# New instruction orders for the first and last sequences of a 32-sequence decoder layer, and where ScalarE's tables are loaded

## The chip, the core and the metric

The kernel runs on one core of a Trainium2 chip. The metric is the device time of one execution in microseconds (us). A core has five engines that each work through their own list of instructions in order: TensorE (PE, matrix products), VectorE (DVE), ScalarE (ACT), GpSimd (POOL) and SyncE (SP), which here only issues transfers. They are tied together by semaphores alone.

## The reference, cut to what matters

For each of 32 sequences of 128 tokens and 512 channels, one decoder layer is computed:

```
x = x + Wo( groupnorm(rwkv(LN(x))) * silu(g) )      # projections r, k, v, g of token-shift mixes of LN(x)
x = x + softmax(q k^T / 4) v                        # q = LN(x), k = v = ctx, 32 heads over 8 KV heads
x = x + FFN(LN(x))                                  # W1, gelu, W2; inputs and weights quantised to
                                                    # MXINT8 in blocks of 32, LN and output in bf16
```

The linear attention works in chunks with a per-head decay; its state runs inside one sequence only, so the sequences do not depend on each other. They share the weights: five float32 matrices of 512x512, and W1 (2048x512) and W2 (512x2048), which the kernel quantises itself, once, in 16 pieces.

## The kernel before

The whole kernel is a software pipeline over sequences n = 0 to 31. Each engine's block defines small helpers (one step of one sequence: `stats_q(n)`, `project("r", n, ...)`, `scores_max(n, i)`) and then calls them in an order that is written out by hand: a long straight list for the first sequences, a loop `for n in range(10, 27)` for the middle, and another straight list for the last ones. At one time about six sequences are in flight. In one pass of the loop the engines do steps of sequences n, n - 1, ... n - 5. Nothing sorts the work at run time: an instruction that waits holds up everything behind it on its engine.

The steps that the prediction speaks of, with their lines in the kernel before:

- Load and quantise a weight piece (16 pieces, 512 KB each, in two buffers `wst`): SP `load_w12(n)` (L200) waits until piece n - 2 is quantised (`dve_w_q`); VectorE `w12_scale(n)` takes block maxima (L1739, L1660, L1666, L1667); GpSimd `w12_scaled(n)` multiplies (L3292); VectorE `w12_quantise(n)` rounds (L1747, L1751); SP `w12_turned(n)` transposes by DMA (L266).
- First LayerNorm: VectorE `stats_q(n)`, `norm_mv("q", n)`; ScalarE `rstd_log`, `rstd_exp` (a logarithm and an exponential) and `normalise_q(n)` (L2529, writes `xx`); TensorE `turn_x(n)` transposes it (L516, waits for `act_xn`); ScalarE `x_turned(n)`; VectorE `differences(n)` (L1553); then `mixed` for k and v on VectorE, for r and g on GpSimd; then the projections.
- The decay masks `wm`, once: `distances(i)` (L1758), ScalarE `decays(i)`, GpSimd `bonuses(i)` (L3301), `bonus_added(i)` (L1764).
- Projection out: VectorE `scaled_y`, `gated_y` (L1597, L1601), TensorE `project_out(n)` (L599), VectorE `first_sum(n)` (L1608). Then the cross-attention: `normalise_x` (L2536), `turn_queries` (L605), `queries_x` (writes `qdense`, L2612), `scores_max` (L614), `maxima` (L1614), `scores_x`, `weights_x`, `values_x`, `out_odd` (L2642), `turn_sums`, `turn_out`, `normalise_o` (L1630, writes `x2`, whose buffer must have been stored two sequences before).
- Feed-forward: `hidden...` steps, `up(n, j)` (L654), `gelu(n, j)`, `gelu_max`, `gelu_pow2`, `gelu_scale` (GpSimd, L3282), `gelu_round`, `gelu_quantised` (L1719), a DMA transpose, `down(n, i)` (L663), `second_out`, `last_sum`, `store`.

ScalarE can hold one table of functions at a time. The steps with a logarithm or exponential need `TABLE_EXP`, `gelu` and `gate_tanh` need `TABLE_GELU`; the plain copies and scalings (`normalise_q`, `queries_x`, `x_turned`, `out_odd`) run under either. The loads are written into the order as `e.preload_act_table_set(...)`.

In the middle loop of the kernel before, ScalarE's order around the second LayerNorm reads:

```
gelu(n - 4, 1); out_odd(n - 3); <load TABLE_EXP>
rstd_log("x", n - 2); rstd_exp("x", n - 2); normalise_x(n - 2)
rstd_log("q", n); rstd_exp("q", n); normalise_q(n); queries_x(n - 2); x_turned(n)
<load TABLE_GELU>; gate_tanh(n - 1); gate_in(n - 1)
```

## Time and profile before

| | |
|---|---|
| Three timed runs | 1359.17, 1360.65, 1353.01 us; median 1359.17 |
| Profiled execution, span from first to last instruction | 1355.6 us |
| TensorE busy | 1249.7 us (92%), mean granted clock 0.968 |
| VectorE busy | 1134.3 us (84%) |
| ScalarE busy | 823.1 us (61%) |
| GpSimd busy | 636.6 us (47%) |
| DMA | 97.09 MB, mean 72 GB/s |

The page gives the profiled execution by its span alone; no other time of it is shown. "PE" is TensorE's products, "PEld" its weight loads, which overlap with them. L-numbers are lines of the kernel before; helpers are called for every sequence, so a line stands for one step of all sequences. "Idle before" is the time in which the engine had nothing to do ahead of a row, with what ended it. A granted clock of 1.00 is 2.4 GHz and 0.50 is 1.2 GHz.

### The profile page before, as it was taken

The numbers are of one execution on the slowest core, as the hardware profiler recorded it, in microseconds if no ns is written. First come the engines' busy times: TensorE is split into PE (matmuls) and PEld (weight loads), VectorE is DVE, ScalarE is ACT, GpSimd is POOL, SyncE is SP. The second block draws the span as 40 slices with busy tenths as digits, with TensorE's granted clock in tenths as the row PEclk, the third lists the DMA queues.
The fourth block names the chain that finished last, engine by engine and source line by source line (L and its number), as shares of the span: only waits on it lengthen the run. The fifth ranks groups of instructions, "written<-read, shape, count | busy, mean of one in ns | idle before, by whom it ended". The sixth has DMA issues, their size and how long they took to land.

```text
span 1355.6 us, 34643 instructions
## 1 busy us (share of the span) xinstructions
PE 1249.7 (92%) x13352; PEld 797.8 (59%) x13352; DVE 1134.3 (84%) x1960; ACT 823.1 (61%) x1577; POOL 636.6 (47%) x700
## 2 busy tenths in 40 slices
PE   1677989999999999999999999999999999999744
PEld 1564666656666666566666666666666666666411
DVE  5889978888888887888888888888888888888875
ACT  1334475766666666666666666667666666666641
POOL 3756444544445445544445455444445454443322
PEclk8789999999999999999999999999999999999976
DMA  9335312222222223222212233222212322221212
GB/s 323 101 95 136 67 39 73 70 71 57 51 57 61 63 67 70 70 70 49 56 50 64 65 70 70 71 70 50 56 52 64 63 71 69 70 59 38 67 49 51
DMA packets 137332, 97.09 MB, mean 72 GB/s; under 512 B 108113, under 2 KB 110161, under 8 KB 136401
## 3 DMA queue, kind: packets, MB, share of 16 engines
q1 hardware_dynamic: 137168, 94.87, 27.8%
q8 instruction: 107, 1.75, 0.6%
q14 instruction: 57, 0.46, 0.1%
HBM read 37.16 MB, written 8.39 MB: 34 GB/s over the span
## 4 chain that ended last, share of the span: by engine, by line
PE 79%; DVE 10%; issue 4%; DMA 2%; POOL 2%; ACT 1%; SPq 1%; POOLq 0%; DVEq 0%; ACTq 0%
PE bank_b L547 15%; PE bank_y L599 8%; PE bank_a L547 8%; PE bank_y L663 7%; PE bank_a L537 7%; PE rt L566 5%; PE rt L614 4%; PE rt L627 4%; PE bank_o L633 4%; PE bank_b L654 4%; PE bank_a L654 4%; PE bank_o L593 2%; PE bank_y L585 2%; PE bank_y L580 1%; DVE negm L1614 1%
## 5 line engine op out<-in xcount | busy, mean ns | idle before, releaser
L3282 POOL TENSOR_TENSOR gmem<-gmem,unit_g 128x1024 bf16<-128x1024 bf16 x64 | 124.1, 1940 | 214.1 <-DVE unit_g L1667 214.1
L1614 DVE TENSOR_REDUCE negm<-rt 128x16 f32<-128x2048 f32 x64 | 146.2, 2284 | 2.3 <-PE rt L614 1.5
L663 PE MATMUL bank_y<-w2q,gmem 128*128 128x512 bf16 x512 | 122.4, 393 | 19.3 <-DMA gmem<-gmem 19.3
L2626 ACT ACTIVATE pT<-rt 128x2048 f32<-128x2048 f32 x64 | 120.0, 1875 | 28.1 <-PE rt L627 20.3
L547 PE MATMUL bank_a<-mix_r,w_Wr 128*128 128x128 f32 x1024 | 124.3, 280 | 5.6 <-POOL mix_r L3241 5.6
L547 PEld LDWEIGHTS bank_a<-mix_r,w_Wr 128*128 128x128 f32 x1024 | 118.5, 194 | 16.1 <-issue 10.1
L547 PE MATMUL bank_b<-mix_k,w_Wk 128*128 128x128 f32 x1024 | 122.1, 278 | 5.2 <-DVE mix_k L1560 5.2
L3273 POOL TENSOR_TENSOR gt<-gt,yT 128x512 f32<-128x512 f32 x32 | 41.1, 1285 | 181.0 <-ACT yT L2604 181.0
L547 PEld LDWEIGHTS bank_b<-mix_k,w_Wk 128*128 128x128 f32 x1024 | 120.5, 196 | 7.2 <-issue 7.2
L547 PE MATMUL bank_b<-mix_g,w_Wg 128*128 128x128 f32 x1024 | 122.0, 278 | 0.0
L547 PEld LDWEIGHTS bank_b<-mix_g,w_Wg 128*128 128x128 f32 x1024 | 118.6, 194 | 2.0 <-issue 1.6
L599 PE MATMUL bank_y<-w_Wo,yT 128*128 128x512 f32 x256 | 115.4, 593 | 1.3 <-DVE yT L1601 1.3
L537 PE MATMUL bank_a<-w_Wv,mix_v 128*128 128x512 f32 x256 | 115.5, 594 | 0.1
L1585 DVE TENSOR_TENSOR att<-rt,wm 128x1536 f32<-128x1536 f32 x64 | 112.1, 1751 | 2.9 <-PE bank_y L585 1.4
L663 PEld LDWEIGHTS bank_y<-w2q,gmem 128*128 128x128 bf16 x512 | 50.1, 100 | 86.6 <-issue 27.5
L3266 POOL TENSOR_TENSOR gh<-gt,half_ln 128x512 f32<-128x512 f32 x32 | 52.3, 1635 | 77.3 <-DVE gt L1592 77.3
L2578 ACT ACTIVATE gt<-bank_b,half_bg 128x128 f32<-128x128 f32 x128 | 36.5, 370 | 79.7 <-PE bank_b L547 79.7
L537 PEld LDWEIGHTS bank_a<-w_Wv,mix_v 128*128 128x128 f32 x256 | 48.2, 190 | 61.9 <-issue 59.9
L566 PEld LDWEIGHTS rt<-rz,kT 32*64 32x64 f32 x3072 | 63.1, 131 | 34.0 <-issue 25.2
L3237 POOL TENSOR_SCALAR mix_r<-xx,all_columns 128x128 f32<-128x128 f32 x128 | 49.6, 406 | 65.0 <-DVE xx L1553 65.0
L1719 DVE SCALAR_TENSOR_TENSOR gmem<-gmem,pow_g 128x1024 bf16<-128x1024 f16 x64 | 79.2, 1238 | 1.1
L599 PEld LDWEIGHTS bank_y<-w_Wo,yT 128*128 128x128 f32 x256 | 48.2, 190 | 54.0 <-issue 49.1
(205 smaller groups left out, 2829.8 us busy)
## 6 DMA issues: line engine op xcount, KB each, us to landing
qx<-qdense SPq DMA_DIRECT2D x64, 224.0 KB, 3.1
context<-ctx SPq DMA_DIRECT2D x32, 384.0 KB, 3.3
xin<-x SPq DMA_DIRECT2D x32, 256.0 KB, 3.2
gmem<-w SPq DMA_DIRECT2D x16, 512.0 KB, 4.0
out<-x SPq DMA_DIRECT2D x32, 256.0 KB, 2.9
vp<-vz SPq DMA_DIRECT2D x32, 128.0 KB
odense<-oT SPq DMA_DIRECT2D x128, 32.0 KB, 1.9
pT<-Wv SPq DMA_DIRECT2D x1, 1024.0 KB, 8.1
```

The lines of the kernel that those rows point to most:

```text
L537: done = e.matmul(bank_a[:, :], mix["v"][:, c, :], wt["Wv"][:, c, :], start=(c == 0), stop=(c == KT - 1))
L547: done = e.matmul(bank[:, m * T:(m + 1) * T], wt[f"W{name}"][:, c, m * P:(m + 1) * P], mix[name][:, c, :], start=(c == 0), stop=(c == KT - 1))
L566: done = e.matmul(rtb(g)[HALF * side:HALF * side + HALF, at:at + (q1 - q0) * HALF], kT[rows32, m, HALF * keys:HALF * keys + HALF], rz[rows ...
L599: done = e.matmul(bank_y[:, :], yT[:, c, :], wt["Wo"][:, c, :], start=(c == 0), stop=(c == KT - 1))
L614: done = e.matmul(rtb(g)[:, jj * 2 * T:(jj + 1) * 2 * T], qdense[rows32, 2 * i + jj, :], kd[n % 2][rows32, :, :], start=True, stop=True)
L654: done = e.matmul(bank[:, :], hqT[:, c, :], w1q[:, 4 * j:4 * j + 4, c, :], start=(c == 0), stop=(c == KT - 1))
L663: done = e.matmul(bank_y[:, :], gqT[:, t, :], w2q[:, t, :], start=(t == 0), stop=(t == FT - 1))
L1585: e.tensor_tensor(att[:, :, :, :, :].rearrange("p g m k t -> p g (m k t)"), rt[:, :].rearrange("p (g n) -> p g n", g=4)[:, :, 0:6 * HALF], ...
L1614: e.tensor_reduce(negm[:, 0:H].rearrange("p (g a j) -> p g j a", g=4, a=2)[:, :, 2 * i:2 * i + 2, :], rt[:, :].rearrange("p (g j a s) -> p ...
L1719: e.scalar_tensor_tensor(blocks(half), blocks(half.bitcast(FP16)), MAGIC16, per_block(pow2[f"g{i}"], 32), ALU.subtract, ALU.mult).then_inc ...
L2626: e.activation(pT[:, :, :].rearrange("p g n -> p (g n)"), rt[:, :], ACT.Exp, scale=float(D) ** -0.5).then_inc(sem(f"act_ex{i}"), 1)
L3282: e.tensor_tensor(blocks(half), blocks(half), per_block(unit[f"g{i}"], 32), ALU.mult).then_inc(sem(f"pool_gsc{i}"), 1)
```

## The change

Every helper's arithmetic is as before; no instruction on the data is added or taken away. Changed are:

- the straight lists ahead of and behind the loops, on all five engines;
- the ranges of the loops (TensorE 7 to 26, VectorE 9 to 26, ScalarE 9 to 27, GpSimd 8 to 31, SP 10 to 27; before 10 to 26 on all), each beginning at another step of the pass. Taken round in a circle, the order of the steps in the pass is the same as before on all engines;
- the places of ScalarE's table loads. In the kernel before a load stands right ahead of the first step that needs the table, after it right behind the last step that needed the other one. This holds inside the loop too. Over the whole kernel there are 12 loads fewer;
- one added wait, of `project_out(0)` for the load of `Wo`.

```diff
@@ SP, start
-            load_x(0)
-            load("masks", masks[:, :], masks_in)
-            load("columns", all_columns[:, :, :], columns)
-            load("heads", per_head[:, :], heads)
-            load_w12(0)
             load_w12(1)
-            load("Wv", wv_rows, weights["Wv"])
-            load("b1", b1row[:, :], b1)
-            for k in ROWS:
-                load("rows", row[k][:, :], rows[k])
+            load("Wo")
+            load_row("bo")
             load_x(1)
...
+            load("Wv")
+            load("Wk")
             load_w12(2)
             load_w12(3)
+            load("Wr")
             w12_turned(1)
+            w12_turned(0)
+            load_row("ffn_ln_w")
+            load("Wg")
             load_w12(4)
...
@@ ScalarE, middle loop
-            for n in range(10, 27):
+            for n in range(9, 28):
...
                 e.preload_act_table_set(TABLE_GELU)
                 gelu(n - 4, 0)
                 gelu(n - 4, 1)
+                e.preload_act_table_set(TABLE_EXP)
                 out_odd(n - 3)
-                e.preload_act_table_set(TABLE_EXP)
                 rstd_log("x", n - 2)
                 rstd_exp("x", n - 2)
                 normalise_x(n - 2)
                 rstd_log("q", n)
                 rstd_exp("q", n)
+                e.preload_act_table_set(TABLE_GELU)
                 normalise_q(n)
                 queries_x(n - 2)
                 x_turned(n)
-                e.preload_act_table_set(TABLE_GELU)
                 gate_tanh(n - 1)
                 gate_in(n - 1)
```

VectorE, from the rounding of weight piece 2 back to the first LayerNorm's statistics, before (`amax_w`, `pow_w`, `unit_w` are block maxima of a weight piece, `hz` and `hw` the two buffers of quantised pieces, `xx` the result of `differences(0)`):

```order
L1739 TENSOR_REDUCE amax_w<-gmem 128x32
L1660 TENSOR_SCALAR amax_w<-amax_w 128x32
L1666 TENSOR_SCALAR pow_w<-amax_w 128x32
L1667 TENSOR_SCALAR unit_w<-amax_w 128x32
L1521 BN_STATS stats_q<-xin 128x6
L1529 BN_AGGR mv_q<-stats_q 128x2
L1532 TENSOR_SCALAR shift_q<-mv_q 128x1
L1521 BN_STATS stats_q<-xin 128x6
L1747 TENSOR_SCALAR gmem<-gmem 128x1024
L1751 SCALAR_TENSOR_TENSOR hz<-gmem,pow_w 128x1024
L1553 TENSOR_TENSOR xx<-xT 128x512
```

and after:

```order
L1374 BN_AGGR mv_q<-stats_q 128x2
L1377 TENSOR_SCALAR shift_q<-mv_q 128x1
L1366 BN_STATS stats_q<-xin 128x6
L1374 BN_AGGR mv_q<-stats_q 128x2
L1377 TENSOR_SCALAR shift_q<-mv_q 128x1
L1592 TENSOR_SCALAR gmem<-gmem 128x1024
L1596 SCALAR_TENSOR_TENSOR hz<-gmem,pow_w 128x1024
L1592 TENSOR_SCALAR gmem<-gmem 128x1024
L1596 SCALAR_TENSOR_TENSOR hw<-gmem,pow_w 128x1024
L1398 TENSOR_TENSOR xx<-xT 128x512
```

Before, the maxima of pieces 2 and 3 and the rounding of pieces 0, 1 and 2 stand ahead of `xx`; after, only pieces 0 and 1 do (their maxima stand further up), and `distances(1)` and `bonus_added(0)` come later too.

ScalarE in the middle loop, before, from the load that follows `out_odd`:

```order
L2961 ACT_TABLE_LOAD
L2510 ACTIVATE logv_x<-mv_x,eps 128x1
L2517 ACTIVATE rstd_x<-logv_x 128x1
L2521 ACTIVATE shift_x<-shift_x,rstd_x 128x1
L2536 ACTIVATE xq<-x_1,shift_x,rstd_x 128x512
L2510 ACTIVATE logv_q<-mv_q,eps 128x1
L2517 ACTIVATE rstd_q<-logv_q 128x1
L2521 ACTIVATE shift_q<-shift_q,rstd_q 128x1
L2529 ACTIVATE xx<-xin,shift_q,rstd_q 128x512
L2612 ACTIVATE qdense<-rt 128x512
L2561 ACTIVATE xT<-bank_o 128x4x128
L2970 ACT_TABLE_LOAD
```

and after:

```order
L2728 ACT_TABLE_LOAD
L2449 ACTIVATE oT<-bank_o 128x512
L2317 ACTIVATE logv_x<-mv_x,eps 128x1
L2324 ACTIVATE rstd_x<-logv_x 128x1
L2328 ACTIVATE shift_x<-shift_x,rstd_x 128x1
L2343 ACTIVATE xq<-x_1,shift_x,rstd_x 128x512
L2317 ACTIVATE logv_q<-mv_q,eps 128x1
L2324 ACTIVATE rstd_q<-logv_q 128x1
L2328 ACTIVATE shift_q<-shift_q,rstd_q 128x1
L2735 ACT_TABLE_LOAD
L2336 ACTIVATE xx<-xin,shift_q,rstd_q 128x512
L2419 ACTIVATE qdense<-rt 128x512
```

The first load has moved from behind `oT` (`out_odd`) to ahead of it, the second from behind `xT` to ahead of `xx` (`normalise_q`).

VectorE shortly before the last `project_out`, before (`yT` is first `scaled_y(31)`, then `gated_y(31)`):

```order
L1689 SCALAR_TENSOR_TENSOR hz<-hz,pow_h 128x512
L1719 SCALAR_TENSOR_TENSOR gmem<-gmem,pow_g 128x1024
L1655 TENSOR_REDUCE amax_g<-gmem 128x32
L1597 TENSOR_TENSOR yT<-bank_y,gt 128x512
L1660 TENSOR_SCALAR amax_g<-amax_g 128x32
L1666 TENSOR_SCALAR pow_g<-amax_g 128x32
L1667 TENSOR_SCALAR unit_g<-amax_g 128x32
L1601 TENSOR_TENSOR yT<-yT,gh 128x512
```

and after:

```order
L1442 TENSOR_TENSOR yT<-bank_y,gt 128x512
L1529 TENSOR_SCALAR hz<-hz 128x512
L1446 TENSOR_TENSOR yT<-yT,gh 128x512
L1534 SCALAR_TENSOR_TENSOR hz<-hz,pow_h 128x512
L1564 SCALAR_TENSOR_TENSOR gmem<-gmem,pow_g 128x1024
L1500 TENSOR_REDUCE amax_g<-gmem 128x32
```

The two steps of sequence 31 now stand ahead of the last rounding of the hidden layer and of the quantising of sequence 28's gelu.

## Rows read from the trace of the kernel before

**Rows 1.** Head of the page: span, and busy time of each engine.
```profile
span 1355.6 us, 34643 instructions
...
PE 1249.7 (92%) x13352; PEld 797.8 (59%) x13352; DVE 1134.3 (84%) x1960; ACT 823.1 (61%) x1577; POOL 636.6 (47%) x700
...
```

**Rows 2.** Windows: stretch, length, busy us (count) of PE, PEld, DVE, ACT, POOL; PEclk.
```profile
0.00:204.00 204.00, 144.62 (x1573) 103.78 (x1573) 168.62 (x252) 88.98 (x176) 107.80 (x112) 0.88 0.46 128
600.00:900.00 300.00, 300.00 (x3265) 193.99 (x3263) 254.88 (x457) 200.78 (x391) 147.65 (x168) 1.00 0.25 62
1254.00:1356.00 102.00, 60.70 (x435) 26.02 (x430) 72.75 (x125) 41.61 (x67) 28.96 (x19) 0.80 0.24 55
```

**Rows 3.** Timeline of VectorE, 0 to 90 us: start, length, engine, line, operation, [idle before].
```profile
6.17 2.67 DVE L1772 TENSOR_SCALAR per_head<-per_head 128x48 f32<-128x48 f32 x1 [1.25 <-ACT per_head L2672]
...
17.08 2.80 DVE L1751 SCALAR_TENSOR_TENSOR hz<-gmem,pow_w 128x1024 bf16<-128x1024 f32 x1
...
20.52 1.23 DVE L1751 SCALAR_TENSOR_TENSOR hw<-gmem,pow_w 128x1024 bf16<-128x1024 f32 x1
...
32.24 1.22 DVE L1739 TENSOR_REDUCE amax_w<-gmem 128x32 f32<-128x1024 f32 x1 [8.83 <-DMA gmem<-w]
...
40.76 0.69 DVE L1553 TENSOR_TENSOR xx<-xT 128x512 f32<-128x512 f32 x1 [0.66 <-ACT xT L2561]
...
58.20 0.69 DVE L1572 TENSOR_TENSOR vz<-bank_a,bv_row 128x512 f32<-128x512 f32 x1 [2.44 <-PE bank_a L537]
...
88.19 0.69 DVE L1608 TENSOR_TENSOR x<-bank_y,xin 128x512 f32<-128x512 f32 x1 [3.63 <-PE bank_y L599]
```

**Rows 4.** Timeline of the DMA-issuing queue, 0 to 30 us.
```profile
19.91 5.98 SPq L266 DMA_TRANSPOSE w1q<-hz  x1
...
25.94 1.05 SPq L200 DMA_DIRECT2D gmem<-w  x2
```

**Rows 5.** Timeline of TensorE, 0 to 60 us.
```profile
45.67 5.48 PE L547 MATMUL bank_a<-mix_r,w_Wr 128*128 128x128 f32 x32 [5.57 <-POOL mix_r L3241]
```

**Rows 6.** Timeline of ScalarE, one pass of the middle loop.
```profile
712.78 0.60 ACT L2642 ACTIVATE oT<-bank_o 128x512 f32<-128x512 f32 x1 [2.55 <-PE bank_o L633]
...
713.39 1.28 ACT L2961 ACT_TABLE_LOAD   x1
...
714.69 0.29 ACT L2510 ACTIVATE logv_x<-mv_x,eps 128x1 f32<-128x1 f32 x1
...
716.80 0.29 ACT L2510 ACTIVATE logv_q<-mv_q,eps 128x1 f32<-128x1 f32 x1 [0.35 <-DVE mv_q L1529]
...
717.75 0.81 ACT L2529 ACTIVATE xx<-xin,shift_q,rstd_q 128x512 f32<-128x512 f32 x1
...
718.47 0.58 ACT L2612 ACTIVATE qdense<-rt 128x512 f32<-128x512 f32 x1
...
720.80 1.28 ACT L2970 ACT_TABLE_LOAD   x1
```

**Rows 7.** Timeline of TensorE, same pass.
```profile
719.49 0.66 PE L516 MATMUL bank_o<-masks,xx 128*128 128x128 f32 x4
...
720.08 1.15 PE L614 MATMUL rt<-context,qdense 32*128 32x256 f32 x16
```

**Rows 8.** Timeline of ScalarE, then TensorE, an earlier pass.
```profile
526.09 0.82 ACT L2529 ACTIVATE xx<-xin,shift_q,rstd_q 128x512 f32<-128x512 f32 x1
...
527.37 0.66 PE L516 MATMUL bank_o<-masks,xx 128*128 128x128 f32 x4
```

**Rows 9.** Timeline of the last 100 us: VectorE three, ScalarE one.
```profile
1270.45 2.30 DVE L1719 SCALAR_TENSOR_TENSOR gmem<-gmem,pow_g 128x1024 bf16<-128x1024 f16 x1
...
1273.80 0.68 DVE L1597 TENSOR_TENSOR yT<-bank_y,gt 128x512 f32<-128x512 f32 x1
...
1315.16 0.69 DVE L1630 TENSOR_TENSOR x<-bank_o,rden 128x512 f32<-128x512 f32 x1 [1.09 <-DMA out<-x]
...
1280.96 1.28 ACT L3192 ACT_TABLE_LOAD   x1
```

More of the change, by code:

```diff
@@ L1105, in _ @@
+            for n in range(7, 27):
                 e.wait_ge(sem("dve_ze0"), n - 3)
@@ L1780, in _ @@
             w12_quantise(1)
[L1781 to L1788 removed]
+            differences(0)
+            distances(1)
+            mixed(0, "v")
+            w12_scale(2)
+            mixed(0, "k")
+            w12_quantise(2)
+            w12_scale(3)
+            bonus_added(0)
+            w12_scale(4)
             w12_quantise(3)
[L1790 removed]
@@ L2276, in _ @@
+            up_out(25, 2, bank_a)
+            gelu_round(25, 0)
+            denominators(26)
+            differences(29)
+            residual(24)
+            maxima(27, 0)
+            mixed(29, "v")
             normalise_o(26)
-            maxima(27, 1)
+            decayed(28, 1)
             stats_f(26)
+            gate(28)
+            gelu_quantised(25, 0)
+            gelu_max(25, 1)
             norm_mv("f", 26)
-            maxima(27, 0)
+            scaled_y(28)
+            gated_y(28)
```

2255 lines of the change are left out of this document (948 added, 1307 removed).

## The prediction

> **What bounds the kernel now.** I read the page's head first. TensorE is busy 1249.7 of 1355.6 us, VectorE 1134.3 [rows 1]. The reader is to ask where the missing 106 us of TensorE lie. The windows answer: there are three stages, each with its own limit [rows 2]. From 600 to 900 us TensorE is busy 300.00 of 300: it alone sets the pace, VectorE has 15% to spare. In the first 204 us TensorE is busy 144.62, which leaves 59.4 us idle, and VectorE 168.62: VectorE, which quantises the weights beside its usual work, is nearer to its limit. In the last 102 us TensorE idles 41.3 us and VectorE 29.3: no engine is full, and the chain of sequence 31 sets the end. The amount of TensorE work is the same in both kernels, so the new time is the old one less the idle time taken out of head and tail, plus whatever idle time appears in the middle, where each microsecond that TensorE waits is a microsecond of the kernel.
>
> The sum is made against the span of 1355.6 us. The page shows no other time of that execution; the three timed runs lie between 1353.01 and 1360.65, so I add the sum to their median, 1359.17, and keep some 3 us for that spread. This measurement can tell about 0.5% (6.8 us) from no change.
>
> **The head: less idle time on VectorE.** VectorE's timeline shows waits of 1.25, 8.83, 0.66, 2.44 and 3.63 us on the way to the first `first_sum` [rows 3]. The largest is for weight piece 2: the SP queue issues seventeen other transfers, then the transpose of piece 0 holds it from 19.91 to 25.89, and only then come the loads of pieces 2 and 3, for which VectorE waits until 32.24 [rows 3, 4]. Sequence 0's LayerNorm stands behind those pieces on VectorE, so `xx` starts at 40.76 and TensorE's first projection at 45.67 [rows 3, 5]. In the new order, pieces 2 and 3 are loaded ahead of any transpose, with b1, three rows and Wg behind them, and the LayerNorm stands behind pieces 0 and 1 alone. What is only moved gains nothing, since VectorE has to do it anyway; what counts are the waits. 8.83 + 0.66 go, because piece 2 is now issued as soon as piece 0 is quantised. That was at 19.88 here (`hz`, 17.08 + 2.80) and should be near 19; with the 6.3 us from 25.94 to 32.24 it lands by 25.3, and VectorE, which first has `xx`, `distances(1)` and `mixed(0, "v")` to do, asks for it at about 26 (an estimate). The 1.25 goes, since piece 0's maxima now stand ahead of the rates. New are a wait for piece 0 to land and one for ScalarE's rstd ahead of the second `norm_mv`, which I estimate at 1.2 us together. That is 9.5 us. Of the other two waits, 2.44 + 3.63, I take half, 3.0. Head: -12.5 us. TensorE then starts near 26 to 28 us instead of 45.67, which is more than VectorE's gain, so VectorE stays the limit and not TensorE. Bounds: 4 us, if other waits take half of it and the later weight pieces come late (each load still waits for the piece two before); 20 us, which is the whole shift of the first projection.
>
> One cost is in this already: a VectorE operation can be held for as long as a GpSimd one runs. `hz` took 2.80 us at 17.08 and its twin `hw` 1.23 at 20.52, and the 48 wide `per_head` took 2.67 [rows 3]. The new order has as many such pairs, at other places; I count 0, with 2 us either way.
>
> **The middle: the table load that moved.** The loop's steps keep their order on every engine, but on ScalarE both loads inside the pass have moved. The first, of 1.28 us at 713.39, goes ahead of `oT` (712.78), where ScalarE was idle for 2.55 us: it is hidden, and brings `logv_x` forward, which nobody waits for, as the next step `logv_q` is held until 716.80 by VectorE anyway [rows 6]. The second, at 720.80, stood where ScalarE then had nothing to do. It now stands between `shift_q` and `xx` (717.75), with `qdense` behind it. So `xx` ends at 717.75 + 1.28 + 0.81 = 719.84 instead of 718.56. TensorE's `turn_x` needs it and started at 719.49 [rows 7]: there was 0.93 us in hand in this pass, 0.46 in the pass at 527.37 [rows 8]. Those are the ends of nine passes that I looked at, seven of them above 0.78; I take 0.8. The new wait is 1.28 - 0.8, or 0.5 us. Nothing catches it up: the input of `logv_q` comes from VectorE, whose list hangs on this pass's `project_out`, so the whole pass slides. `qdense` ends 0.6 after `xx`, at 720.4, and `scores_max` starts behind `turn_x` at 720.08 + 0.5: covered by 0.1. The ScalarE loop has 19 passes (9 to 27): 19 x 0.5 = +9.5 us. Bounds: 0, if a slack that the trace doesn't show takes it; 19 x 1.28 = 24.3, if the slack in front of `turn_x` is not there.
>
> The row of 713.39 is followed by `logv_x` at 714.69, 0.02 after the load ends, and it starts 0.01 after `oT` [rows 6]. The Trainium skill (ScalarE: Activation LUTs, What ACT_TABLE_LOAD costs) gives 1283 ns for the load and another 1380 ns of drain, 2.66 us for a switch. The trace shows the first and not the second. By the page the wait in each pass would be 1.9 us and the middle would lose 36 us; I go by the rows.
>
> **The tail.** Four pieces, each read from a wait or an order. (a) `scaled_y(31)` (the `yT` row) is now ahead of `gmem` and `amax_g`, which filled the time from 1270.45 to 1273.80 [rows 9]; part of these 3.35 us is GpSimd's own arrival, so I take 2.4. (b) The load ahead of the last LayerNorm x, 1.28 us at 1280.96, stood behind `out_odd` on the chain; now it is done earlier: 1.3. (c) `normalise_o(31)` waited 1.09 us for the store of sequence 29 [rows 9]; `down(29, 1)` now stands ahead of `up(30)`, so that store is earlier: 1.1. (d) `gelu_quantised(30, 0)` has moved behind `hidden(31)`, and `second_out(30)` behind the last maxima: 0.7. Tail: -5.5 us. The two `down(30)` halves now stand behind `up(31)`; they run while TensorE waits for the last gelu, which it did before too. Bounds: 0 and 10.
>
> **Sum.** -12.5 + 9.5 - 5.5 = -8.5 us. 1359.2 - 8.5 = 1350.7 us.
>
> **The rivals.**
>
> A, the middle stays free: something ahead of `turn_x` has slack that hides the moved load. For it: TensorE's ends are modelled, and `turn_x` is never seen waiting in the middle. Against: 0.5 to 0.9 us in hand against 1.28. Time: 1359.2 - 18 = 1341.
>
> B, the head gives little: the loads of later pieces, which still wait two by two for VectorE, put the saved 9 us back as waits further on, and the middle costs its 9.5. For it: between 40 and 80 us VectorE's one long wait is the 2.44, so it has no reserve for a late piece. Against: the DMA queue is lightly loaded after 30 us. Time: 1359.2 - 4 + 9.5 - 4 = 1360.7, no change.
>
> C, slower: the moved load falls on TensorE in full, in every pass, and in the passes outside the loop as well, where the same load now stands ahead of `normalise_q` or `queries_x`. Its place is `turn_x`, its price 1.28 x 27 sequences = 34.6 us, and it decides from the point where the slack ahead of `turn_x` is used up by the wait itself. Time: 1359.2 - 18 + 34.6 = 1375.8. Against: the 0.8 to 0.9 us in hand is regular.
>
> D, both ends give more. Of VectorE's 35.4 idle us in the head (204 - 168.62) the five waits make 16.8; the other 18.6 shrink too. Time, with the upper bound of the head and 8 for the tail: 1359.2 - 20 + 9.5 - 8 = 1340.7.
>
> E, slower by a drain: a switch of tables costs about two of its bars, because work ahead of the load has to drain first. In this kernel the wait of `turn_x` would be 2 x 1.28 - 0.8 = 1.8 us in 19 passes, and the time 1359.2 - 18 + 33.4 = 1374.6. Against: the row of 713.39 starts 0.01 after the one ahead of it. It is the page's rule quoted above, with the bar taken from the trace.
>
> **How the numbers follow.** Forecast 0.45, A 0.15, B 0.22, C 0.06, D 0.10, E 0.02. The forecast's own range is 1344 to 1357. For 8 in 10 the range reaches down to A and D and up past B: 1339 to 1364. Faster by over 0.5% means below 1352.4: A, D and six tenths of the forecast, 0.53. Within 0.5% (to 1366): the rest of the forecast and most of B, 0.38. Slower: C, E and a little of B, 0.09.
>
> **What the profile after would show.** Head: `xx` of `differences(0)` near 21 us, the first projection before 30, no wait of VectorE over 3 us for a weight piece, and TensorE's idle time in the first 204 us near 47 instead of 59.4. Middle: TensorE no longer 300 of 300 us busy but some 296, with `turn_x` waiting for ScalarE's `xx` about 0.5 us a pass, and a pass 0.5 us longer. Tail: no wait of `normalise_o(31)` for a store, and about 36 us idle from the point where TensorE was last full. The forecast is wrong if `turn_x` never waits in the middle, or if VectorE shows new waits for `amax_w` between 40 and 140 us.

## The result: slower by 0.7%, and the profile after

| | before | after |
|---|---|---|
| Median of the timed runs | 1355.91 us | 1364.51 us |
| Ratio, 95% interval | | 1.0066 [1.0047, 1.0085] |
| Span of the profiled execution | 1355.6 us | 1362.1 us |
| TensorE idle in it | 105.9 us | 110.5 us |

The forecast was 8.5 us less; measured are some 9 us more. The time lies 0.5 us above the range of 1339 to 1364, and on the other side of no change. The forecast was added to a median of three runs, 1359.17; the seventeen runs of the kernel before have 1355.91, so measured against that kernel the miss of the range is nearer to 4 us.

The head of the page after, which answers [rows 1], and the same three windows as [rows 2] (the last one ends with the span):

```profile
span 1362.1 us, 34631 instructions
...
PE 1251.6 (92%) x13352; PEld 799.4 (59%) x13352; DVE 1132.3 (83%) x1960; ACT 796.3 (58%) x1565; POOL 651.5 (48%) x700
...
```

```profile
0.00:204.00 204.00, 158.85 (x1735) 111.95 (x1736) 171.16 (x269) 88.31 (x184) 112.27 (x115) 0.92 0.51 135
600.00:900.00 300.00, 292.07 (x3161) 188.44 (x3161) 250.31 (x445) 192.84 (x378) 143.75 (x162) 1.00 0.23 58
1254.00:1362.00 108.00, 71.89 (x531) 31.73 (x521) 79.22 (x141) 46.16 (x76) 31.35 (x20) 0.84 0.24 57
```

In the first 204 us TensorE idles 45.2 us instead of 59.4. From 600 to 900 us it idles 7.9 us instead of none. Fixed windows mislead where the whole program shifts, so the stages are better cut at an event that both kernels have: the start of VectorE's `first_sum` of sequences 0, 9, 24, 27 and 31. (The last window shows it: it idles 36.1 us after, which is what the prediction's marker for the tail asked for, but it holds another part of the work than before.) Here from `first_sum(9)` to 24, before and after (15 passes of the loop; columns as above):

```profile
442.61:1015.24 572.63, 571.01 (x6248) 367.50 (x6256) 486.64 (x870) 380.27 (x736) 277.30 (x315) 1.00 0.26 63
```

```profile
429.94:1019.12 589.18, 572.11 (x6248) 367.59 (x6256) 490.39 (x870) 377.45 (x737) 279.23 (x315) 1.00 0.24 61
```

The length less TensorE's busy time gives its idle time:

| TensorE idle, us | to first_sum(0) | to 9 | to 24 | to 27 | to 31 | to the end |
|---|---|---|---|---|---|---|
| before | 46.2 | 16.5 | 1.6 | 0.6 | 6.6 | 34.2 |
| after | 32.5 | 18.1 | 17.1 | 3.0 | 8.3 | 31.5 |
| after, GELU load put back | 28.8 | 15.4 | 2.3 | 2.9 | 8.3 | 31.6 |
| after, store first | 29.2 | 15.9 | 7.6 | 3.2 | 7.7 | 33.6 |
| after, GELU load one later | 33.2 | 17.7 | 18.1 | 4.7 | 8.9 | 31.8 |
| after, EXP load put back | 33.9 | 16.9 | 16.2 | 3.4 | 8.2 | 32.2 |
| after, all loads late | 32.7 | 19.9 | 0.8 | 5.1 | 9.3 | 32.5 |
| before, both loads early | 42.2 | 19.4 | 17.9 | 0.5 | 4.8 | 34.7 |
| new head alone | 34.5 | 16.0 | 2.8 | 0.2 | 4.4 | 36.6 |
| new head alone, again | 33.1 | 16.6 | 2.9 | 1.1 | 6.6 | 34.5 |
| before, transfers of the head alone | 34.8 | 17.2 | 6.1 | 0.0 | 4.5 | 34.4 |
| new tail alone | 41.1 | 17.2 | 0.8 | 3.9 | 8.3 | 32.3 |

Each row is one execution, and not always a middling one: those of "GELU load put back" and "store first" are the fastest executions of their kernels. Kernels with the same lists differ by up to 6 us in the first column and by 2 to 3 in the second and the last. Read so, the head gains some 12 us and the middle loses 15 us in 15 passes. The last three columns lose 1.4 us together: 4.1 ahead of the last `first_sum`, with 2.7 won behind it.

The head after. SP issues, which answer [rows 4], VectorE, which answer [rows 3], and TensorE's first projection [rows 5]:

```profile
20.59 2.19 SPq L209 DMA_DIRECT2D gmem<-w  x2
...
22.82 0.43 SPq L201 DMA_DIRECT2D w_Wr<-Wr  x1
...
23.30 1.59 SPq L275 DMA_TRANSPOSE w1q<-hw  x1
```

```profile
22.34 0.68 DVE L1398 TENSOR_TENSOR xx<-xT 128x512 f32<-128x512 f32 x1
...
26.11 1.21 DVE L1584 TENSOR_REDUCE amax_w<-gmem 128x32 f32<-128x1024 f32 x1
```

```profile
29.78 6.05 PE L549 MATMUL bank_a<-mix_r,w_Wr 128*128 128x128 f32 x32 [6.04 <-DMA w_Wr<-Wr]
```

`xx` starts at 22.34, piece 2 is read at 26.11 without a wait, and the first projection starts at 29.78 instead of 45.67, now waiting for `Wr`, which has moved behind the pieces.

One pass of the middle. ScalarE and TensorE, which answer [rows 6, 7]:

```profile
711.97 0.29 ACT L2328 ACTIVATE shift_q<-shift_q,rstd_q 128x1 f32<-128x1 f32 x1
...
712.28 1.28 ACT L2735 ACT_TABLE_LOAD   x1
...
713.58 0.81 ACT L2336 ACTIVATE xx<-xin,shift_q,rstd_q 128x512 f32<-128x512 f32 x1
...
714.30 0.58 ACT L2419 ACTIVATE qdense<-rt 128x512 f32<-128x512 f32 x1
```

```profile
714.54 0.63 PE L518 MATMUL bank_o<-masks,xx 128*128 128x128 f32 x4 [0.68 <-ACT xx L2336]
...
715.10 1.15 PE L618 MATMUL rt<-context,qdense 32*128 32x256 f32 x16
...
739.82 1.02 PE L658 MATMUL bank_a<-w1q,hqT 128*128 128x512 bf16 x4 [1.15 <-DMA hqT<-hz]
```

The load starts 0.02 us behind `shift_q` and `xx` 0.02 behind the load, as in [rows 6]. The Trainium skill (ScalarE: Activation LUTs, What ACT_TABLE_LOAD costs) adds 1380 ns of drain to a switch; this trace again shows none. `turn_x` waits 0.68 us for `xx`, where 0.5 was forecast. The last row is what was not forecast: `up` waits 1.15 us for `hqT`. The waits between 306 and 1200 us (waiting engine, what, for whom, sum, times, longest), after and then before, where `turn_x` does not appear:

```profile
DVE x L1475 <- DMA out<-x: 19.1, 17, 2.3
...
PE bank_o L518 <- ACT xx L2336: 9.9, 18, 0.9
...
PE bank_a L658 <- DMA hqT<-hz: 8.0, 7, 1.8
```

```profile
DVE x L1630 <- DMA out<-x: 10.0, 13, 2.0
...
PE bank_a L654 <- DMA hqT<-hz: 2.3, 2, 1.2
```

The tail after: the last `scaled_y(31)`, `gelu_quantised(28, 0)`, `first_sum(31)` and `normalise_o(31)` on VectorE, and ScalarE ahead of the last `xq`, which answer [rows 9]:

```profile
1279.54 0.68 DVE L1442 TENSOR_TENSOR yT<-bank_y,gt 128x512 f32<-128x512 f32 x1
...
1281.55 1.21 DVE L1564 SCALAR_TENSOR_TENSOR gmem<-gmem,pow_g 128x1024 bf16<-128x1024 f16 x1
...
1286.61 0.69 DVE L1453 TENSOR_TENSOR x<-bank_y,xin 128x512 f32<-128x512 f32 x1 [2.19 <-PE bank_y L603]
...
1323.26 0.68 DVE L1475 TENSOR_TENSOR x<-bank_o,rden 128x512 f32<-128x512 f32 x1
```

```profile
1289.21 1.28 ACT L2922 ACT_TABLE_LOAD   x1
1290.51 0.81 ACT L2343 ACTIVATE xq<-x,shift_x,rstd_x 128x512 f32<-128x512 f32 x1
```

The same `first_sum(31)` and `xq` before:

```profile
1279.32 0.69 DVE L1608 TENSOR_TENSOR x<-bank_y,xin 128x512 f32<-128x512 f32 x1 [0.38 <-PE bank_y L599]
```

```profile
1283.21 0.81 ACT L2536 ACTIVATE xq<-x,shift_x,rstd_x 128x512 f32<-128x512 f32 x1
```

### The profile page after: what moved, and what is told of

Its sections match the earlier page's. It is cut to its first block, busy times and chain, and to the rows that moved or that the text cites. A ratio compares the mean times of both kernels' runs of the same rounds, so it can differ in the third digit from the quotient of the medians.

```text
span 1362.1 us, 34631 instructions
## 1 busy us (share of the span) xinstructions
PE 1251.6 (92%) x13352; PEld 799.4 (59%) x13352; DVE 1132.3 (83%) x1960; ACT 796.3 (58%) x1565; POOL 651.5 (48%) x700
## 4 chain that ended last, share of the span: by engine, by line
PE 48%; DVE 22%; issue 10%; DMA 7%; POOL 5%; ACT 4%; SPq 2%; ACTq 0%; POOLq 0%; DVEq 0%
PE bank_b L549 11%; PE bank_y L603 6%; PE bank_a L549 5%; PE bank_a L539 5%; PE rt L618 3%; PE rt L631 3%; DVE att L1430 3%; DVE amax_g L1500 2%; PE bank_a L658 2%; PE bank_b L658 2%; PE bank_o L595 2%; PE rt L568 2%; DMA xin<-x 2%; PE bank_o L637 2%; DMA hqT<-hz 2%
## 5 line engine op out<-in xcount | busy, mean ns | idle before, releaser
L2433 ACT ACTIVATE pT<-rt 128x2048 f32<-128x2048 f32 x64 | 119.9, 1873 | 22.6 <-PE rt L631 16.5
L667 PEld LDWEIGHTS bank_y<-w2q,gmem 128*128 128x128 bf16 x512 | 50.0, 100 | 73.2 <-issue 17.2
L568 PEld LDWEIGHTS rt<-rz,kT 32*64 32x64 f32 x3072 | 63.8, 132 | 40.5 <-issue 22.2
L568 PE MATMUL rt<-rz,kT 32*64 32x128 f32 (+2 forms) x3072 | 73.9, 282 | 11.9 <-DVE att L1430 7.1
L658 PE MATMUL bank_b<-w1q,hqT 128*128 128x512 bf16 x256 | 67.7, 388 | 16.8 <-DMA hqT<-hz 14.7
```

The costliest lines, as they stand in the source:

```text
L568: done = e.matmul(rtb(g)[HALF * side:HALF * side + HALF, at:at + (q1 - q0) * HALF], kT[rows32, m, HALF * keys:HALF * keys + HALF], rz[rows ...
L658: done = e.matmul(bank[:, :], hqT[:, c, :], w1q[:, 4 * j:4 * j + 4, c, :], start=(c == 0), stop=(c == KT - 1))
L667: done = e.matmul(bank_y[:, :], gqT[:, t, :], w2q[:, t, :], start=(t == 0), stop=(t == FT - 1))
L2433: e.activation(pT[:, :, :].rearrange("p g n -> p (g n)"), rt[:, :], ACT.Exp, scale=float(D) ** -0.5).then_inc(sem(f"act_ex{i}"), 1)
```

## The experiments

Fifteen kernels were run, one of them twice, in four groups, each beside runs of the kernel before on the same chip. Ratios are to the kernel before, with 95% intervals of some 2 to 3 us to either side. In the cuts below, the lines with semaphore waits are left out.

### The middle: which load, and by which way

**The loop's GELU load put back** behind `x_turned`, all else as after:

```diff
-                e.preload_act_table_set(TABLE_GELU)
                 normalise_q(n)
                 queries_x(n - 2)
                 x_turned(n)
+                e.preload_act_table_set(TABLE_GELU)
```

> The changed kernel, with the load of TABLE_GELU in ScalarE's middle loop (19 passes) put back from ahead of normalise_q to behind x_turned. Theory T (this one load makes the whole loss of the middle, half of it as the wait of turn_x, half of it by way of qdense, the SP queue, the store and normalise_o): TensorE idle from 306 to 1200 us falls from 26.5 to under 5 us, no wait of turn_x for xx, time about 22 us under the changed kernel: 1342 us, 0.990 of the kernel before. Rival R (the load costs only the 9.9 us of turn_x; the other 13 come from the phase in which the new head enters the loop): 10 us less, about 1354.5, and the waits of up for hqT stay.

Measured: 1346.48 us, ratio 0.9941 [0.9922, 0.9959]. The idle time of TensorE between `first_sum(9)` and `first_sum(24)` falls from 17.1 to 2.3 us, `turn_x` no longer waits, and of the waits for `hqT` (9.4 us after) 5.1 us are left.

One line of the loop turns the whole change from slower to faster.

**The loop's EXP load put back** behind `out_odd`:

```diff
-                e.preload_act_table_set(TABLE_EXP)
                 out_odd(n - 3)
+                e.preload_act_table_set(TABLE_EXP)
                 rstd_log("x", n - 2)
```

> The changed kernel, with only the load of TABLE_EXP in the loop put back from ahead of out_odd to behind it; the load of TABLE_GELU stays ahead of normalise_q. Theory T: nothing changes, 1364 us within 3, TensorE idle from 306 to 1200 us near 26. Rival (the early load of TABLE_EXP holds out_odd and with it the sums and normalise_o): some 10 us less.

Measured: 1365.13 us, ratio 1.0089 [1.007, 1.0107], middle idle 16.2 us. This load is hidden at either place, as the prediction had it.

**SP issues the store ahead of the queries' copy**, all else as after:

```diff
-                queries_spread(n - 2)
                 store(n - 5)
+                queries_spread(n - 2)
```

> The changed kernel, with store(n - 5) ahead of queries_spread(n - 2) in the SP loop, so that a late qdense no longer holds the store. Theory T: VectorE's waits of normalise_o for the store (19.1 us) and TensorE's for hqT (9.4 us) go, those of turn_x (9.9 us) stay: TensorE idle from 306 to 1200 us about 13, time about 1353. Rival R: the waits for hqT have another cause, nothing changes: 1364.

Measured: 1351.67 us, ratio 0.9975 [0.9956, 0.9994]. The middle's idle time falls from 17.1 to 7.6 us, and what stays is mostly the wait of `turn_x`:

```profile
PE bank_o L518 <- ACT xx L2336: 9.2, 18, 0.8
```

**The kernel before with both loads of the loop placed as after:**

```diff
                 gelu(n - 4, 1)
+                e.preload_act_table_set(TABLE_EXP)
                 out_odd(n - 3)
-                e.preload_act_table_set(TABLE_EXP)
...
                 rstd_exp("q", n)
+                e.preload_act_table_set(TABLE_GELU)
                 normalise_q(n)
                 queries_x(n - 2)
                 x_turned(n)
-                e.preload_act_table_set(TABLE_GELU)
```

> The kernel before, with both loads in ScalarE's loop (17 passes) placed as in the changed kernel; head and tail as they were. Theory T: the middle loses the same per pass as in the changed kernel, 22.6 x 17/19 = 20 us: 1376 us, 1.015 of the kernel before. Rival R: only 0.5 a pass, 9 us: 1365.

Measured: 1371.68 us, ratio 1.0139 [1.0119, 1.0158]: 19 us for the places of two loads in a loop of 17 passes, with nothing else changed. By the trial of the EXP load, the GELU load is the one that costs. The middle idles 17.9 us, where the kernel after has 17.1.

**The loop's GELU load one instruction later**, between `normalise_q` and `queries_x`:

```diff
-                e.preload_act_table_set(TABLE_GELU)
                 normalise_q(n)
+                e.preload_act_table_set(TABLE_GELU)
                 queries_x(n - 2)
```

> The kernel after, with the loop's load of the GELU table moved by one instruction: behind normalise_q instead of ahead of it. turn_x of TensorE then gets xx as early as in the kernel before, but queries_x (qdense) is still 1.28 us late. Theory T (half of the middle's loss goes through turn_x, the other half through the late qdense, which holds the SP queue's copy of the queries and the store behind it, and so normalise_o and the hidden layer's transpose): turn_x no longer waits for xx, the waits of up for hqT and of normalise_o for the store stay, TensorE's idle time between 306 and 1200 us falls from 26.6 to 15 to 19, and the time is 7 to 11 us under the kernel after, ratio to the kernel before about 1.000. Rival R1 (all of the loss starts at turn_x, and the waits for hqT follow from it): idle time 306 to 1200 as with the load wholly back, 10.8, ratio 0.994. Rival R2 (only qdense counts): idle stays at 22 or more, ratio 1.005.

Measured: 1365.52 us, ratio 1.0086 [1.0066, 1.0106]. Theory T fell in this form, and so did R1: nothing was won. The wait is still there under another name, at the next step of TensorE:

```profile
PE rt L618 <- ACT qdense L2419: 10.1, 19, 0.8
...
PE bank_a L658 <- DMA hqT<-hz: 9.2, 8, 1.8
```

`qdense` is as late as in the kernel after, and `scores_max`, which needs it, waits 10.1 us in 19 passes where `turn_x` waited 9.9 in 18. So R2 is right in kind: what counts is when `qdense` is done, and an early `turn_x` only shortens the time until the same wait.

### Where the way leads

The rows show the second half of the loss. SP in one pass, before and after, and the VectorE steps around it:

```profile
719.08 1.19 SPq L235 DMA_DIRECT2D qx<-qdense  x2
...
720.31 0.59 SPq L284 DMA_DIRECT2D out<-x  x1
...
739.91 1.23 SPq L273 DMA_TRANSPOSE hqT<-hz  x1
```

```profile
714.90 1.17 SPq L244 DMA_DIRECT2D qx<-qdense  x2
...
716.13 0.60 SPq L293 DMA_DIRECT2D out<-x  x1
...
737.25 1.23 SPq L282 DMA_TRANSPOSE hqT<-hz  x1
```

```profile
710.68 0.69 DVE L1608 TENSOR_TENSOR x<-bank_y,xin 128x512 f32<-128x512 f32 x1 [0.22 <-PE bank_y L599]
...
723.62 0.68 DVE L1630 TENSOR_TENSOR x<-bank_o,rden 128x512 f32<-128x512 f32 x1
```

```profile
705.12 0.69 DVE L1453 TENSOR_TENSOR x<-bank_y,xin 128x512 f32<-128x512 f32 x1 [0.22 <-PE bank_y L603]
...
720.25 0.69 DVE L1475 TENSOR_TENSOR x<-bank_o,rden 128x512 f32<-128x512 f32 x1 [1.52 <-DMA out<-x]
```

Counted from `first_sum` (710.68 and 705.12): the queries' copy is issued 8.40 us after it before and 9.78 after the change, since it stands at the head of SP's list until `qdense` is there. The store behind it follows at 9.63 and 11.01. `normalise_o` writes the `x2` buffer that this store reads; before, it did not wait in this pass; after, it waits 1.52 us and runs at 15.13 instead of 12.94. Over the middle this wait was there before too, 10.0 us in 13 passes, and is 19.1 us in 17 passes after. The transpose of the hidden layer, which hangs on it, comes at 32.13 instead of 29.23, and `up` waits 1.15 us. In this pass, a load of 1.28 us has become 2.9 us of lateness six steps on. It does not reach TensorE in every pass: in the middle `up` waits 8 times, 9.4 us in all, against 2.3 us before. With the store first, the transpose comes at 29.59 in this pass though `qdense` is still late, VectorE's wait for the store is gone, and 7.6 of 17.1 us are left.

### The head

**The new lists of the first sequences alone**, loop and tail as before; run twice:

```diff
@@ all engines: straight list ahead of the loop
-(the kernel before's)
+(the kernel after's)
```

> The new lists of the first sequences alone on all engines; from the loop on, steps and table loads as in the kernel before. The prediction's head term, -12.5 us, and TensorE's idle time in the first 204 us, which fell from 59.4 to 45.2 (14.2): if the head's gain comes whole to the end, the time is 12 to 15 us under the kernel before, ratio 0.989 to 0.991, with the idle time between 306 and 1200 us near the 3.9 of before. Rival: the gain is given back in the middle, because sequences in flight start closer together and VectorE or the stores have less reserve: idle 306 to 1200 above 8, ratio above 0.994.

> The new lists of the first sequences alone, once more, to stand beside the two others of this group: 0.989 to 0.993 of the kernel before.

Measured: 1341.74 us, ratio 0.9908 [0.989, 0.9927], and 1342.96 us, 0.9913 [0.9896, 0.993]. The head's gain comes whole to the end. Of all the kernels run, this one is the fastest.

**Pieces 2 and 3 issued ahead of the transpose**, all else as before:

```diff
-            w12_turned(0)
             load_w12(2)
             load_w12(3)
+            w12_turned(0)
```

> The kernel before, with one edit: SP issues the loads of weight pieces 2 and 3 ahead of the transpose of piece 0 (5.98 us) instead of behind it. It tests the prediction's step that the wait of 8.83 us for piece 2 goes and that the end gains by it. Theory H1 (that wait is VectorE time lost): piece 2 lands near 26.2, the wait shrinks to about 2.9 us, xx starts near 35 instead of 40.76, the first first_sum about 5 us earlier than 86 to 88, ratio 0.996. Rival H2 (the saved time is lost again at the later pieces or at the projections, so that only the early place of the first LayerNorm counts): first first_sum within 2 us of before, ratio 0.999 or more.

Measured: 1354.28 us, ratio 0.9973 [0.9957, 0.9989], but `first_sum(0)` at 88.32, as before. The issue moved from 25.94 to 19.68 and the data came no earlier. VectorE's wait, then the line of the loads of weight pieces between 15 and 40 us (KB each, median us from issue to landing) of this kernel, of before and of after:

```profile
33.00 1.22 DVE L1739 TENSOR_REDUCE amax_w<-gmem 128x32 f32<-128x1024 f32 x1 [9.82 <-DMA gmem<-w]
```

```profile
gmem<-w SPq DMA_DIRECT2D x2, 512.0 KB, 13.1
```

```profile
gmem<-w SPq DMA_DIRECT2D x2, 512.0 KB, 6.7
```

```profile
gmem<-w SPq DMA_DIRECT2D x3, 512.0 KB, 3.8
```

From 20 to 30 us the DMA engines moved some 420 GB/s: `Wo`, `Wg`, `Wk` and `Wr`, 1 MB each, were ahead of the pieces. `Wr`, issued at 10.08, landed 21.7 us later, at 31.8, and the pieces right behind it at 32.8. So with these matrices ahead the wait is one for bytes, and the transpose's place changes nothing; whether it would count with the bytes gone was not run. `first_sum(0)` is where H2 had it, for a reason that neither theory had. Its ratio, 0.999 or more, was missed: the ratio says 0.3% faster where the trace, of the slowest of twelve executions, shows no gain in any stage. I draw nothing from it.

**The first LayerNorm ahead of pieces 2 and 3 on VectorE**, all else as before:

```diff
-            bonus_added(0)
-            w12_scale(2)
-            w12_scale(3)
             stats_q(0)
             norm_mv("q", 0)
             stats_q(1)
-            w12_quantise(2)
+            bonus_added(0)
             differences(0)
+            w12_scale(2)
+            w12_scale(3)
+            w12_quantise(2)
             w12_quantise(3)
```

> The kernel before, with one edit: on VectorE the statistics of the first LayerNorm and differences(0) stand ahead of the maxima of weight pieces 2 and 3 instead of behind them; the loads are as before. Theory H1: TensorE's first projection starts near 32 us instead of 45.67, but VectorE still waits for piece 2, now about 7 us behind differences(0), and does the same work after it; the gain at the first first_sum is the part of the wait that differences(0) and mixed fill, 2 to 4 us, ratio 0.997 to 0.999. Rival H2 (the late start of the projections was the limit, not VectorE's waits): the first first_sum comes 9 us or more earlier, ratio 0.993 or less.

Measured: 1355.11 us, ratio 0.9981 [0.9965, 0.9998], `first_sum(0)` at 85.75. `xx` started at 26.29 instead of 40.76, and TensorE's first projection did not move:

```profile
45.32 6.48 PE L547 MATMUL bank_a<-mix_r,w_Wr 128*128 128x128 f32 x32 [19.70 <-POOL mix_r L3241]
```

It waits for GpSimd, where `mixed(0, "r")` stands behind the scaling of pieces 2 and 3. So H1's gain came, 2.4 us at `first_sum(0)`, which is within the scatter of single executions, but not by H1's early projection; H2 fell.

**Transfers alone**, all else as before: `Wk`, pieces 2 and 3, `Wr`, the transpose, `Wg`:

```diff
-            load("Wg", wt["Wg"][:, :, :], weights["Wg"])
             load("Wk", wt["Wk"][:, :, :], weights["Wk"])
-            load("Wr", wt["Wr"][:, :, :], weights["Wr"])
-            w12_turned(0)
             load_w12(2)
             load_w12(3)
+            load("Wr", wt["Wr"][:, :, :], weights["Wr"])
+            w12_turned(0)
+            load("Wg", wt["Wg"][:, :, :], weights["Wg"])
```

> The kernel before with SP's head changed alone: Wk, then weight pieces 2 and 3, then Wr, the transpose of piece 0, Wg; before: Wg, Wk, Wr, the transpose, then the pieces. With only the transpose put behind, the pieces were issued 6.3 us earlier and still landed at 33 us, behind 400 to 440 GB/s of other transfers. Theory H3 (piece 2 waits for the matrices in front of it in the DMA engines, not for its issue): with 2 MB less ahead of it, it lands between 24 and 28 us, VectorE's wait falls from 8.83 to 1 to 4 us, xx starts at 33 to 36 instead of 40.76, the first first_sum at 81 to 84 instead of 86 to 88, ratio 0.995 to 0.998. Rival (the transposes slow it down whatever stands ahead): piece 2 lands after 30 us.

Measured: 1350.0 us, ratio 0.9953 [0.9936, 0.9971], `first_sum(0)` at 79.90. H3 is confirmed, with `xx` at 34.45 and `first_sum(0)` even 1 us ahead of its range: with 2 MB less in front of it, piece 2 is there at 25.93.

```profile
25.93 1.22 DVE L1739 TENSOR_REDUCE amax_w<-gmem 128x32 f32<-128x1024 f32 x1 [3.63 <-DMA gmem<-w]
```

Three lines on the transfer queue give about half of the head's gain.

**The same with the LayerNorm first on VectorE and the mixes first on GpSimd:**

```diff
@@ VectorE as in the LayerNorm's trial, SP as in the one above, GpSimd:
+            mixed(0, "r")
             w12_scaled(2)
-            w12_scaled(3)
-            mixed(0, "r")
             mixed(0, "g")
+            w12_scaled(3)
```

> The kernel with SP's head changed as in the one before this, and the first LayerNorm and differences(0) ahead of the maxima of pieces 2 and 3 on VectorE, and GpSimd's mixed(0, r) ahead of the scaling of piece 2 and mixed(0, g) ahead of that of piece 3. Theory H4 (the head's gain needs the three together: transfers, VectorE's and GpSimd's order): TensorE's first projection near 31 to 34 us instead of 45.67, the first first_sum at 76 to 80, as in the kernel after, ratio 0.990 to 0.993. Rival (the rest of the head's lists carries the gain): first first_sum at 82 or later, ratio 0.995 or more.

Measured: 1351.91 us, ratio 0.997 [0.9958, 0.9983], first projection at 31.03, `first_sum(0)` at 83.36. H4 fell: the first projection is nearly as early as in the kernel after, and the head is no better than with the transfers alone. So the other half of the head's gain is in the rest of the new lists. VectorE's time up to `first_sum(9)` says of what kind it is. With the transfers alone VectorE idles 63.8 us there, 9.0 less than before, and is busy 369.4, as before; with the new head alone it idles 66.8 and is busy 362.1 (again: 66.2 and 364.3). The transfers alone take away the waits, and the rest of the lists makes the same instructions shorter. Which of its moves does that stays open.

### The tail

**The new lists of the last sequences alone:**

```diff
@@ all engines: straight list behind the loop
-(the kernel before's)
+(the kernel after's)
```

> The new lists of the last sequences alone; head and middle loop as in the kernel before. TensorE's idle time from 1200 us to the end fell from 41.3 to 37.2: by that the tail gives 4.1 us, ratio 0.997. Theory U: ScalarE's loads stand early in these lists too, which costs what it costs in the loop, some 1 us in each of the sequences that the straight lists of the tail hold at full pace (4 to 7 of them, here between 1100 and 1254 us), so the tail alone is worth between -2 and +3 us, ratio 0.9985 to 1.002. The prediction's own term: -5.5 us, ratio 0.996.

Measured: 1356.49 us, ratio 1.002 [1.0006, 1.0034]. TensorE idles 3.9, 8.3 and 32.3 us in the last three stages, against 0.6, 6.6 and 34.2 before: 2 us gained behind the last `first_sum`, and more lost ahead of it. The longest wait there, which the kernel after has too and the kernel before does not, is TensorE's in `values_x` for ScalarE's `pT`:

```profile
PE bank_o L807 <- ACT pT L4330: 2.2, 1, 2.2
```

**All loads as late as they can be**, in head and tail too:

```diff
@@ ScalarE, every straight list, as here:
             rstd_exp("x", 28)
-            e.preload_act_table_set(TABLE_GELU)
             out_odd(27)
             normalise_x(28)
+            e.preload_act_table_set(TABLE_GELU)
             gelu(26, 1)
```

> The kernel after with every load of a ScalarE table right ahead of the first step that needs it, in the straight lists of head and tail as in the loop; the order of all else is as after. Theory U (early loads cost in the tail's lists as in the loop, and the 9 us that TensorE idled between 1000 and 1254 us with the loop's load alone put back come from them): idle time between 306 and 1200 us plus that of 1200 to 1254 falls by 6 to 9 us against the kernel with only the loop's GELU load put back, which measured 0.9941 of before; ratio 0.987 to 0.990. Rival V (those waits come from the order of the other steps, not from the loads): no change against 0.9941, within 2 us. Against both: the last LayerNorm's load is on the chain again, at most 1.3 us.

Measured: 1351.23 us, ratio 0.9968 [0.9952, 0.9985], against 0.9941 with the loop's load alone put back; the intervals overlap. Theory U fell: the early loads are not what costs in the tail's lists, since with late ones the last three columns add up to 46.9 us of idle time, with early ones to 42.8 to 45.4. That leaves rival V, the order of the other steps, by exclusion: its "within 2 us" was missed by 2 us, to the slow side.

**The prediction's pieces (a), (b), (c) by themselves**, on the kernel with the new head alone:

```diff
@@ VectorE
+            scaled_y(31)
+            gated_y(31)
             gelu_quantised(28, 0)
             gelu_max(28, 1)
-            scaled_y(31)
             gelu_pow2(28, 1)
-            gated_y(31)
@@ TensorE
+            project_out(31)
             up(29, 0, bank_a)
             up(29, 1, bank_b)
-            project_out(31)
...
+            down(29, 1)
             up(30, 1, bank_b)
             up(30, 0, bank_a)
-            down(29, 1)
@@ ScalarE
+            e.preload_act_table_set(TABLE_EXP)
             out_odd(30)
-            e.preload_act_table_set(TABLE_EXP)
             rstd_log("x", 31)
```

> New lists of the first sequences, middle and tail as in the kernel before (which measured 0.9908), and in the tail the prediction's pieces (a), (b) and (c) alone, as the prediction meant them: scaled_y(31) and gated_y(31) ahead of gelu_quantised(28, 0) with project_out(31) ahead of up(29, 0) and up(29, 1); the load for the last LayerNorm x ahead of out_odd(30); down(29, 1) ahead of up(30, 1). Theory P (each is on the chain of sequence 31 and the prediction's 2.4, 1.3 and 1.1 us come): 4 to 5 us under it, ratio 0.987 to 0.988; from the last first_sum to the end 76 instead of 78.2. Rival Q (a part that is moved only brings TensorE or ScalarE to the next wait, as in the kernel after, where the last first_sum waited 2.19 us for TensorE although gated_y was done early, and where a GELU load stood on the same chain again): 0 to 2 us, ratio 0.989 to 0.991.

Measured: 1350.11 us, ratio 0.9958 [0.9943, 0.9974], against 0.9908 and 0.9913 without them in two other groups: some 6 us slower. Both theories fell; the pieces cost. VectorE's `scaled_y(31)`, then TensorE's `down(28, 0)`:

```profile
1257.88 0.69 DVE L2634 TENSOR_TENSOR yT<-bank_y,gt 128x512 f32<-128x512 f32 x1 [2.96 <-POOL gt L5539]
```

```profile
1268.17 1.67 PE L853 MATMUL bank_y<-w2q,gmem 128*128 128x512 bf16 x7 [2.21 <-DVE x L2645]
```

(a) makes VectorE wait 2.96 us for GpSimd's `gt`, with the rounding that used to fill this time queued behind it: from `first_sum(27)` to 31 it now takes 152.1 us instead of 148.6. (b) brings nothing, since `down(28)` stands ahead of `turn_queries(31)`. (c) leaves the wait for the store as it was, 1.10 us.

**With (d) too:** `gelu_quantised(30, 0)` behind `hidden(31)`, `down(30)` behind `up(31)`:

```diff
@@ VectorE
-            gelu_quantised(30, 0)
...
             gelu_pow2(30, 1)
+            gelu_quantised(30, 0)
@@ SP
+            hidden_turned(31)
             gelu_turned(30, 0)
-            hidden_turned(31)
@@ TensorE
-            down(30, 0)
...
             up(31, 2, bank_a)
+            down(30, 0)
             down(30, 1)
```

> As the one with (a), (b) and (c), and (d) as well: gelu_quantised(30, 0) behind hidden(31), the transpose of the last hidden layer ahead of that of gelu(30, 0), and both halves of down(30) behind up(31). By the traces the stretch from normalise_o(31) to the end took 40.4 us before and 38.8 after. Theory D: (d) gives these 1.6 us, ratio 0.001 under the kernel with (a) to (c). Rival: down(30, 0) behind up(31) falls on the end instead, nothing or up to 2 us more.

Measured: 1354.28 us, ratio 0.9975 [0.9961, 0.999]; from the last `first_sum` to the end 83.2 us instead of 80.1. The rival is right: (d) costs 2 to 3 us, near to what these ratios can tell apart.

**(b) alone, with `turn_queries(31)` ahead of `down(28)`:**

```diff
@@ TensorE
+            turn_queries(31)
             down(28, 0)
             down(28, 1)
-            turn_queries(31)
@@ ScalarE
+            e.preload_act_table_set(TABLE_EXP)
             out_odd(30)
-            e.preload_act_table_set(TABLE_EXP)
```

> New head, middle and tail as before, and in the tail (b) alone: the load for the last LayerNorm x ahead of out_odd(30), now with turn_queries(31) on TensorE ahead of down(28, 0) and down(28, 1). Theory: the load left the chain in the earlier trial as well, but turn_queries stood behind down(28) on TensorE; with both it starts 1.3 us nearer to the last first_sum (3.5 instead of 4.84 us behind it), and the end comes about 1.2 us earlier, ratio 0.001 under the kernel with the new head alone. Rival: down(28) then holds up scores_max(31), no gain.

Measured: 1346.38 us, ratio 0.9938 [0.9923, 0.9954], in the same group as 0.9913: no gain, rather a loss, though the intervals just overlap. `turn_queries` starts 3.58 us behind `first_sum` instead of 4.84, as expected, and VectorE then waits 5.67 us for `down(28)`:

```profile
1273.08 0.69 DVE L2764 SCALAR_TENSOR_TENSOR o_bf<-bank_y,r_b 128x512 bf16<-128x512 f32 x1 [5.67 <-PE bank_y L853]
```

## Why the prediction was wrong

**The parts add up.** By the ratios, the new head alone: -12 us, twice measured. Loads moved in the loop alone: +19. New tail alone: +3. Together +10; the whole change measured +9. Each ratio is known to some 2 to 3 us, so the parts do not act on each other by more than 4 or 5 us, and each term can be judged by itself.

**The head, -12.5: right in size, and that in part by luck.** The markers held: `xx` at 22.3 (21 forecast), first projection at 29.8 ("before 30"; the working had 26 to 28), idle in the first 204 us 45.2 (47). But the 8.83 us did not go "because piece 2 is now issued as soon as piece 0 is quantised": issued as early and with the same matrices ahead, the piece landed at 33 us. It went because `Wr` and `Wg` are now behind it. And the early LayerNorm, with which the first projection was to move from 45.67, did not move it by itself.

The waits were not the whole either. VectorE runs the same 605 instructions up to `first_sum(9)`, before and after:

```profile
0.00:442.61 442.61, 379.89 (x4093) 252.82 (x4101) 369.84 (x605) 243.60 (x474) 220.20 (x239) 0.95 0.35 92
```

```profile
0.00:429.94 429.94, 379.34 (x4093) 253.77 (x4101) 362.16 (x605) 229.33 (x466) 227.49 (x239) 0.96 0.37 95
```

It idles 67.8 us instead of 72.8 and is busy 362.2 instead of 369.8. Of the 12.7 us by which `first_sum(9)` comes earlier, 5.0 are waits, and 7.7 are shorter instructions (`mix_v`, for one, takes 356 ns instead of 457 in the mean). That is not scatter: the eleven kernels with the new head lists are busy 358.1 to 364.3 us up to there, the seven others 365.8 to 370.9. The step "what counts are the waits" failed there, and so did the count of 0, with 2 us either way, for VectorE operations that are held. VectorE's waits for weight pieces up to 430 us only fell from 9.1 to 7.8 us: the one for piece 0 is 2.97 (1.2 was allowed for it and one more), and between 40 and 140 us there are 2.5 us of them where 0.2 were, which the prediction had named as a sign of being wrong.

**The middle, +9.5: the term that was mis-sized.** Its mechanism was right, its first half was right to the tenth (0.5 us in each of 18 to 19 passes, 9.9 in sum), and its whole was twice that: 15.5 us in the 15 passes between `first_sum(9)` and 24, 1.03 us a pass in the mean, or some 19.6 us for 19 passes (an estimate). By the ratios the loads alone cost 19 us in the 17 passes of the kernel before, and putting the GELU load back won 17 in the 19 passes of the kernel after. The step that failed is "`qdense` ends 0.6 after `xx`, at 720.4, and `scores_max` starts behind `turn_x` at 720.08 + 0.5: covered by 0.1". On TensorE the row bears it out: 715.10 for `scores_max`, 0.2 behind the end of `qdense`. But it asked only TensorE whether it misses `qdense`. The other reader of `qdense` is SP, whose list is in order too: behind the queries' copy stands the store of an earlier sequence, for which VectorE waits, and behind VectorE's step the hidden layer's transpose, for which TensorE waits. That way costs 9.5 of the 17.1 us of idle time, by the trial with the store first. "Nothing catches it up" was right, and it also grows. The upper bound of 24.3 us, drawn from the full 1.28 us, held.

**The tail, -5.5: wrong in sign.** It came to +3 by the ratio of the tail alone, and to +1.4 of idle time in the trace after. The step that failed is the adding up of (a) to (d) as if each wait were a price. Each piece was read off a single wait or order, and each ended at the next one. (a) VectorE was busy while GpSimd's `gt` was under way; without the filling it waits 2.96 us. (b) In the kernel after, a GELU load stands between `rstd_exp` and `normalise_x` of sequence 31: `xq` starts 3.90 us behind `first_sum`, before 3.89. I had looked at the load that left and not at the one that came. (c) `normalise_o(31)` no longer waits for the store there, and still comes 36.65 us behind `first_sum` instead of 35.84. (d) From there to the end the kernel after takes 38.8 us instead of 40.4, which is the one gain, and (d) added to the other three cost 2 to 3. Which moves of the new tail carry its loss ahead of the last `first_sum` stays open.

**The rivals.** None was right. A fell, since `turn_x` waits in 18 passes, and D, since the tail gave nothing. Of C, the place and the direction were: the load does fall on TensorE, by 1.03 of its 1.28 us in the mean, but through two ways, and not in all 27 sequences. B's doubt of the head was not borne out in the time, though late weight pieces did appear. E's drain is not in the rows.

With the middle's 19.6 in place of 9.5 and the tail's +2.5 in place of -5.5, the prediction's own sum would have been +9.6 us; with 17 for the middle, +7.

## What to carry to other kernels

When an instruction is made late, follow every reader of its result, the transfer queue first: a queue in order passes the lateness on to whatever is issued behind it, and that may come back to the bottleneck engine larger than it started. A table load costs nothing where its engine would be idle, so place it behind the last instruction that somebody is waiting for. Before counting a wait as a gain, look at what fills the time beside it, and at what bytes are in front of a transfer, since an earlier issue does not mean an earlier landing.
